# Cross attention 3: two of sixteen banks of maxima per chunk go through SBUF

## What is computed

```python
def _L3_xattn_ref(Q, K, V, mask, Wq, bq, Wk, bk, Wv, bv, Wo, bo):
    ...
    scores = jnp.einsum('bhqd,bhkd->bhqk', q, k) / np.sqrt(D_HEAD).astype(np.float32)
    scores = jnp.where(mask == 0, jnp.float32(-1000000000.0), scores)
    attn = jax.nn.softmax(scores, axis=-1)
    ctx = jnp.einsum('bhqk,bhkd->bhqd', attn, v)
    ctx = ctx.transpose(0, 2, 1, 3).reshape(b, s, h * d)
    return ctx @ Wo.T + bo
```

## Time and profile before

| | us |
|---|---|
| median of 3 runs | 5749.84 (5748.77 to 5754.9) |
| the profiled execution | 5753.69 |
| its span, first to last instruction | 5752.0 |
| stretch of the steady maxima, chunks 14 to 103 | about 4497 to 5431 |
| exponentials of the last pair after it | about 5431 to 5540 |

### The profile page before, as it was taken

One profiled execution on the slowest core, in us unless ns is written; L12 is line 12 of the kernel. 1 busy time (PEld: TensorE's weight loads), 2 busy tenths in 40 slices (PEclk: granted clock), 3 DMA queues, 4 the chain that ended last, 5 costly groups with the idle time before them and its releaser, 6 DMA issues. The chain is left out here.

```text
span 5752.0 us, 67092 instructions
## 1 busy us (share of the span) xinstructions
PE 5158.6 (90%) x26382; PEld 1644.9 (29%) x26382; DVE 3192.3 (56%) x3563; ACT 3458.9 (60%) x3537; POOL 2226.0 (39%) x1118
## 2 busy tenths in 40 slices
PE   8879999999999999889897799998886788888889
PEld 3323333333333333233343311111332111111123
DVE  5687777777777772225522300000257988888723
ACT  4566666666666666511122499999125677777861
POOL 1139899998989899716352000000000000000000
PEclk7889999999999999899998799999895899999999
DMA  1000000000000000000000300000203000000010
GB/s 51 15 1 1 5 1 5 1 5 1 4 5 1 5 1 5 21 22 1 2 0 10 111 22 21 13 10 5 79 25 136 3 11 12 12 14 10 6 46 31
DMA packets 67590, 104.45 MB, mean 18 GB/s; under 512 B 12100, under 2 KB 52134, under 8 KB 65164
## 3 DMA queue, kind: packets, MB, share of 16 engines
q1 hardware_dynamic: 67070, 99.34, 5.2%
q10 hardware_dynamic: 206, 0.83, 0.0%
HBM read 74.58 MB, written 25.43 MB: 17 GB/s over the span
## 5 line engine op out<-in xcount | busy, mean ns | idle before, releaser
L2518 ACT ACTIVATE Pr<-ps,key_bias 128x1024 f32<-128x1024 f32 x816 | 864.6, 1110 | 658.9 <-PE ps L2383 658.8
L2619 DVE TENSOR_REDUCE red<-ps 128x2 f32<-128x1024 f32 (+1 forms) x767 | 904.3, 1180 | 422.9 <-PE ps L2370 422.0
L2720 POOL TENSOR_TENSOR Ps<-Ps,Pr 128x1024 f32<-128x1024 f32 x400 | 943.0, 2358 | 145.0 <-ACT Pr L2518 144.2
L2729 POOL TENSOR_TENSOR Ps<-Ps,Pr 128x1024 f32<-128x1024 f32 x400 | 941.2, 2353 | 0.0
L3354 DVE TENSOR_REDUCE red<-ps 128x1 f32<-128x512 f32 (+3 forms) x1024 | 877.3, 907 | 95.8 <-PE ps L3227 76.0
L3310 ACT ACTIVATE Pr<-ps 128x1024 f32<-128x1024 f32 x816 | 786.2, 1021 | 228.3 <-PE ps L3237 227.4
L2383 PE MATMUL ps<-Q,Kr 64*128 64x512 f32 x3264 | 805.2, 610 | 43.6 <-DVE ps L2343 24.8
L2403 PE MATMUL ps<-Pr,Vc 128*64 128x512 f32 x3264 | 790.1, 605 | 0.0
L3484 ACT ACTIVATE Pr<-ps 128x2048 f32<-128x2048 f32 x467 | 726.2, 2034 | 1.6 <-PE ps L3447 1.6
L2343 DVE CAST ps<-seeds 128x1024 f32<-128x1024 bf16 x499 | 601.1, 1221 | 187.5 <-ACT Pr L2518 172.5
L3227 PE MATMUL ps<-Kp,Q 52*128 52x512 bf16 (+1 forms) x1664 | 442.7, 412 | 171.1 <-DVE red L3354 125.2
(11 more groups left out here) (583 smaller groups left out, 5068.2 us busy)
## 6 DMA issues: line engine op xcount, KB each, us to landing
L_dram_K<-parts SPq DMA_DIRECT2D x26, 384.0 KB, 3.0
Kp<-L_dram_K SPq DMA_DIRECT2D x14, 624.0 KB
L_dram_K<-parts SPq DMA_DIRECT2D x26, 256.0 KB, 2.9
wB<-L_ffn_shares SPq DMA_DIRECT2D x1, 6144.0 KB
w<-L_ffn_experts_w_dram SPq DMA_DIRECT2D x24, 256.0 KB
Kp<-L_dram_K SPq DMA_DIRECT2D x14, 416.0 KB
over<-cross_dram_inverse SPq DMA_DIRECT2D x14, 256.0 KB, 3.8
wB<-L_ffn_shares SPq DMA_DIRECT2D x1, 3584.0 KB, 12.7
```

The lines of the kernel that those rows point to most:

```text
L2518: nc.scalar.activation(Pr[:, t % 4, half].rearrange("p a n -> p (a n)"), ps[:, 2 * half:2 * half + 2, :].rearrange("p a n -> p (a n)"), AC ...
L2619: nc.vector.tensor_reduce(red[:, i // C % 2, q, :, i % C], ps[:, b:b + 2, 0:ctx.keys_in(i % C)], AX, ALU.max).then_inc(*reduced.up())
L2720: nc.gpsimd.tensor_tensor(into, into, src, ALU.add).then_inc(*summed0.up())
L2729: nc.gpsimd.tensor_tensor(into, into, src, ALU.add).then_inc(*summed1.up())
```

## The change

In each chunk from 14 on, one unit of two items is no longer reduced from PSUM: unit 6 in an even chunk, unit 3 in an odd one. ScalarE copies its two banks in fp32 to a tile `beside` in SBUF, which has two slots (`put_aside`), and banks 4 and 5 count as free when this copy is done. The copy stands in ScalarE's queue between the step's two exponentials; where the chunk 14 behind has only three tiles it stands ahead of both or behind both. VectorE takes the maxima from SBUF three units later (`reduce_aside`), with two `tensor_scalar` instructions, one for each item: a maximum with -3e38, whose output goes back to its place and whose accumulator is the maximum over the row.

```diff
+    beside = k.tile(stack, "beside", [128, 2, 2, HALF])
...
+    def aside_unit(i):
+
+        return 6 if (i - LAG) % 2 == 0 else 3
...
     def taken_off(i, u):
 
-        n = act_number(i, u)
-        return copied.at(n + 1) if u in act_units(i) else reduced.at(unit_number(i, u) - n + 1)
+        if i >= LAG and u == aside_unit(i):
+            return aside.at(aside_number(i) + 1)
+        return copied.at(act_number(i, u) + 1) if u in act_units(i) else reduced.at(reduced_number(i, u) + 1)
...
+        def put_aside(g, u):
+            first, n, b = units(g)[u]
+            m, keys = aside_number(g), ctx.keys_in(g % C)
+            nc.scalar.wait_ge(*maxima_mm.at(unit_number(g, u) + 1))
+            if m >= 2:
+                nc.scalar.wait_ge(*aside_reduced.at(2 * (m - 1)))
+            nc.scalar.copy(beside[:, m % 2, :, 0:keys], ps[:, b:b + n, 0:keys]).then_inc(*aside.up())
...
+                    if LAG <= g < N and aside_unit(g) in items and items.index(aside_unit(g)) == half:
+                        put_aside(g, aside_unit(g))
                     if 0 <= j < N:
                         nc.scalar.wait_ge(*scored.at(2 * t + half + 1))
...
+                if LAG <= g < N and aside_unit(g) in items[2:]:
+                    put_aside(g, aside_unit(g))
...
+        def reduce_aside(g):
+            first, n, b = units(g)[aside_unit(g)]
+            m, keys = aside_number(g), ctx.keys_in(g % C)
+            nc.vector.wait_ge(*aside.at(m + 1))
+            for a in range(n):
+                nc.vector.tensor_scalar(beside[:, m % 2, a, 0:keys], beside[:, m % 2, a, 0:keys], -3e38, -3e38, ALU.max, ALU.max,
+                                        accum_out=red[:, g // C % 2, first + a, g % C:g % C + 1]).then_inc(*aside_reduced.up())
...
+                if g >= LAG and u == aside_unit(g):
+                    continue
                 nc.vector.wait_ge(*maxima_mm.at(unit_number(g, u) + 1))
                 if p >= 2 and g % C == 0:
                     nc.vector.wait_ge(*rows_step.at(3 * p - 4))
                 nc.vector.tensor_reduce(red[:, z, first:first + n, g % C], ps[:, b:b + n, 0:ctx.keys_in(g % C)], AX, ALU.max).then_inc(*reduced.up())
+                if g >= LAG and u == aside_unit(g) + 3:
+                    reduce_aside(g)
```

More of the change, by code:

```diff
@@ L3131, in small_softmax @@
         "out_copied", "out_stored0", "out_stored1", "zeroed")
+    aside, aside_reduced = k("scores_aside", "aside_reduced")
     out_stored = (out_stored0, out_stored1)
@@ L3165, in act_number, with aside_number, reduced_number @@
         return sum(len(act_units(x)) for x in range(i)) + sum(x < u for x in act_units(i))
+    def aside_unit(i):
+        return 6 if (i - LAG) % 2 == 0 else 3
+    def aside_number(i):
+        return i - LAG
+    def reduced_number(i, u):
+        n = unit_number(i, u) - act_number(i, u)
+        return n if i < LAG else n - aside_number(i) - (u > aside_unit(i))
     def taken_off(i, u):
-        n = act_number(i, u)
-        return copied.at(n + 1) if u in act_units(i) else reduced.at(unit_number(i, u) - n + 1)
+        if i >= LAG and u == aside_unit(i):
+            return aside.at(aside_number(i) + 1)
+        return copied.at(act_number(i, u) + 1) if u in act_units(i) else reduced.at(reduced_number(i, u) + 1)
     def maxima_at(g, s, steps):
@@ L3358, in dve @@
                 nc.vector.wait_ge(*folded.at(act_number(g + 1, 0)))
-                nc.vector.wait_ge(*reduced.at(unit_number(g + 1, 0) - act_number(g + 1, 0)))
+                nc.vector.wait_ge(*reduced.at(reduced_number(g + 1, 0)))
+                if p:
+                    nc.vector.wait_ge(*aside_reduced.at(2 * aside_number(g + 1)))
                 if p == 0:
```

## The result

The changed kernel takes 5830.4 us (median of 4 runs, 5829.3 to 5831.0), the kernel before, run beside it, 5752.4. The ratio is 1.0136 with a 95% interval of 1.0123 to 1.0149: slower by 78 us. The forecast was 5871 with a range of 5815 to 5915; sign and range held, and the forecast loss of 121 us was half as much again as the measured one.

The account below looks back on a forecast made before the run. VectorE was taken as the bound. Per two chunks, unit 8's delays and slow compares less the covered gap gave +2.94 us; 77 steady chunks made +113, the others +8: +121 on 5749.8, 5871 us, range 5815 to 5915.

Parts of the forecast that it names:

- The bound: In the steady stretch VectorE sets the pace, working 841 of 934 us, with one gap of 0.58 us in 20.32.
- The two gaps: VectorE idles about 0.6 us between units 5 and 7, and about 0.8 us before unit 8, released by ScalarE's copy.
- The fourth case: TensorE has unit 8 in place in time and both gaps close: 5708 us (chance 0.05) or no change (0.05).
- The copy on ScalarE: One added copy per chunk, about 1 us of ScalarE's work, costed at nothing.
- The sum: Steady chunks lose 1.18 us (even) and 1.76 (odd), 2.94 per two; with other chunks +121 us, 5871.
- The compare: Each added VectorE compare takes 0.72 us with its accumulator read (0.47 to 0.84), a pair per chunk 1.44.
- The delay of unit 8: Unit 8 waits for ScalarE's copy, so VectorE starts it 0.32 us later per chunk; odd chunks taken the same.
- The compares were to cover 0.58 us of waiting: In even chunks units 10 and 0 are filled while the compares run, so the 0.58 us gap goes away.
- The chunks at a pair's ends: Seven short last chunks at +0.5 us and six first chunks of a pair at +0.8 us: +8 us.
- the second case: The compare runs at the fast rate, 0.47 us with accumulator: +0.97 us per chunk, 5831 us, chance 0.17.
- both cases: The main forecast, 5871 us with slow compares (chance 0.62), and the second case, 5831 us.

Follow-up runs that it names:

- the copy alone: Kernel before with an unread copy of the same size added on ScalarE in the same place, without any wait: 5755.9 us, ratio 1.0005.
- The last run: Changed kernel with the copy ahead of both exponentials, compares in VectorE's gaps, and products ahead of the even chunk's last unit: 5764.7 us, ratio 1.0020.

## Why the prediction was right, and where its sizes were off

**The bound and the gaps: right.** VectorE was read as bound, but bound in a loop with TensorE over two places for maxima, not by its queue alone. The run without compares shows it most clearly: nothing was gained by the missing reduction. The two gaps forecast in each chunk are where they were put, with the releaser named: 0.48 us (forecast 0.6) and 0.77 (forecast 0.84).

**The fourth case: out.** It needed unit 8 in place by 4922.1, and both things that it named hold it back: the copy, and with the copy early the products.

**The copy on ScalarE: right as placed.** Its cost at nothing is confirmed by the copy alone. The last run shows the cover it lives on.

**The sum.** Forecast +2.94 us per two chunks, measured 22.39 - 20.32 = +2.07, 0.87 less. Times 38.5 the miss is 34 us, most of the 43 between forecast and result. It falls on these terms:
- The compare was taken as 0.65 + 0.07 = 0.72 us and takes 0.605, four times: 0.46 us. Both parts were wrong in kind. The 0.65 was the spacing of singles in a queue that seemed to run without a wait, and an instruction that waits for nothing is spaced by 0.60. The accumulator read doesn't add to it.
- The delay of unit 8 was put at 0.32 us per chunk, 0.64 for two. The run without compares shows 0.32 for two: again 0.32 us too much. From the start of unit 5 to the start of unit 8 the traces have 2.48 us before and 2.64 after. The prediction placed unit 8 of the kernel before at 4922.66, and it starts at 4922.76. The gaps themselves were put 0.19 us too long per chunk.
- The compares were to cover 0.58 us of waiting. They add 1.75 us to the period and not their own 2.42, so they cover 0.67 net, although the 0.27 for the unit that TensorE loads late was not seen: 0.09 us.

Behind the first two stands one misreading. The 19.74 us for 22 reductions contain waits of 0.05 to 0.13 us that the view doesn't list: at 1.13 a double and 0.60 a single they would take 18.6. So the kernel before had already about 1.2 us of hidden waiting in two chunks beside the gap of 0.58, and VectorE was less tightly bound than the prediction read it.

**The chunks at a pair's ends.** Costed at +8 us. From the first reduction of chunk 14 to the last of chunk 103 it is 934.5 us before and 1012.7 after, 78 us more, and 77 x 1.035 = 80: the other chunks gave some 2 us back. The starts of the chunks in the two traces tell which kind was mis-sized. Six short last chunks take 51.0 us before and 53.6 after, 0.43 each, near the 0.5 that was forecast. Six first chunks of a pair take 83.3 and 80.7, 0.43 less each, where 0.8 more was forecast.

**A coincidence to be wary of.** The measured time is within 1 us of the second case, 5831. That case is wrong all the same: it had the compare at 0.47 us, and it takes 0.605, at the slow rate. The run without the accumulator is nearest to that case, and it gives 5794, not 5831. Of the 37 us between them 22 are the compare's own length, 0.33 us and not 0.47 (2 x 77 x 0.14); the other 15 are an error that both cases shared, for the most part unit 8's delay (0.32 x 38.5 = 12). So the nearness of the measured time to 5831 is chance.

## What to carry to other kernels

An engine that is busy nine tenths of a stretch can still be bound by a loop: who frees the buffer, who refills it, and in what order the refill is queued. Before work is moved off it, follow one buffer by the clock from release to release without that work; if the next input arrives no sooner, the gain is zero and the moved work's second half is a pure loss. In such a kernel the order of the refilling engine's queue is the cheaper lever: here one block of products moved by one place gave 0.26%. It is no lever by itself: beside the copy on ScalarE the same move took the period from 20.33 to 20.66 us.

## What the runs showed of the hardware

- A `tensor_scalar` with accumulator output on VectorE is recorded as two instructions. 128x512 fp32 from SBUF takes 677 ns and 0.605 us of the queue with it, 418 ns and 0.33 us without it. The read behind it, 82 ns, lies in the shadow of the next instruction; ScalarE's own takes 192 ns.
- Reading the banks from SBUF buys VectorE nothing: a reduction of 128x1024 fp32 takes 1210 ns from SBUF and 1219 from PSUM.
- A row of the timeline that shows no idle time may hold small waits: the same mix of reductions takes 19.74 us in the loop and would take about 18.6 by the spacing of instructions that wait for nothing.
